# A recurrence solved in rounds: the passages between the rounds reordered on four engines

## What is computed

```python
# x: 6250 x 512, 100000 edges (src, dst), sorted by dst
x = x + gnn(layernorm(x), edges)        # segment sum, two dense layers
x = x + lstm(layernorm(x))              # one sequence of 6250 steps, hidden size 512
# the lstm's step, from h = c = 0:
#   f, i, o = sigmoid([x_t, h] @ W_* + b_*);  g = tanh([x_t, h] @ W_c + b_c)
#   c = f * c + i * g;   h = o * tanh(c)
```

## Time and profile before

| | us |
|---|---|
| median of three runs | 2959.19 (2956.31 to 2973.06) |
| the profiled execution | 2975.87 |
| its span, first to last instruction | 2974.3 |
| `lstm_part` in it | from about 1656 |
| mean granted TensorE clock | 0.942 |

### The profile page before, as it was taken

One profiled execution on the slowest core, in us unless ns is written; L12 is line 12 of the kernel. 1 busy time (PEld: TensorE's weight loads), 2 busy tenths in 40 slices (PEclk: granted clock), 3 DMA queues, 4 the chain that ended last, 5 costly groups with the idle time before them and its releaser, 6 DMA issues. The chain is left out here.

```text
span 2974.3 us, 47816 instructions
## 1 busy us (share of the span) xinstructions
PE 2593.7 (87%) x10746; PEld 1892.8 (64%) x10747; DVE 2149.9 (72%) x5785; ACT 1562.4 (53%) x3986; POOL 998.5 (34%) x1018
## 2 busy tenths in 40 slices
PE   7966888889888888897888799899999799989997
PEld 6845766667667666676666566666666555556654
DVE  7745767767677776676776588777777677778886
ACT  5643444444444444444443566566666477756775
POOL 0245556656566566565553100000000000003333
PEclk9977999989999999898999899999999899999999
DMA  9656777767777777676766766577787666659995
GB/s 240 181 147 193 218 208 226 217 196 222 211 213 217 218 214 215 195 223 197 217 207 194 187 190 177 168 242 237 235 243 237 168 165 168 170 157 253 251 252 148
DMA packets 194203, 611.10 MB, mean 205 GB/s; under 512 B 41822, under 2 KB 47966, under 8 KB 164394
## 3 DMA queue, kind: packets, MB, share of 16 engines
q1 hardware_dynamic: 120432, 370.08, 42.0%
q0 software_dynamic: 73712, 240.39, 29.4%
HBM read 468.71 MB, written 141.62 MB: 205 GB/s over the span
## 5 line engine op out<-in xcount | busy, mean ns | idle before, releaser
L823 POOL DMA_INDIRECT kept<-ln_table,kept x800 | 825.5, 1032 | 569.3 <-DVE shared L1030 324.7
L1518 PE MATMUL acc<-shared,state 128*125 128x512 f32 x2244 | 775.8, 416 | 61.6 <-DVE state L1814 46.2
L864 ACT ACTIVATE shared<-kept 128x512 fp32r<-128x512 f32 x800 | 445.2, 620 | 528.1 <-remote 310.4
L1518 PEld LDWEIGHTS acc<-shared,state 128*125 128x125 f32 x2244 | 401.3, 187 | 197.2 <-ACT acc L1449 64.9
L917 PE MATMUL agg<-shared,onehot 128*125 128x512 f32 x1200 | 431.9, 462 | 27.4 <-DVE shared L1030 18.8
L1359 POOL TENSOR_TENSOR out<-h,lx 125x512 f32<-125x512 f32 x50 | 64.5, 1290 | 1124.2 <-DVE h L1839 1124.2
L1518 PE MATMUL acc<-W_low,state 128*125 128x512 f32 x800 | 315.9, 395 | 0.0
L917 PEld LDWEIGHTS agg<-shared,onehot 128*125 128x125 f32 x1200 | 251.0, 218 | 100.8 <-issue 33.6
L1518 PE MATMUL acc<-last_high,state 128*125 128x512 f32 x748 | 298.8, 399 | 0.0
L1030 DVE TENSOR_TENSOR shared<-kept,shared 128x512 fp32r<-128x512 f32 x400 | 267.9, 689 | 14.9 <-ACT shared L864 6.7
L938 PE MATMUL gps<-Wx_high,zT_high 128*125 128x512 f32 x800 | 225.7, 405 | 49.7 <-ACT zT_high L899 33.7
(11 more groups left out here) (235 smaller groups left out, 4319.5 us busy)
## 6 DMA issues: line engine op xcount, KB each, us to landing
xg<-total_rows SPq DMA_DIRECT2D x100, 896.0 KB
xg<-gate_rows SPq DMA_DIRECT2D x88, 896.0 KB
gate_rows<-gout SPq DMA_DIRECT2D x200, 224.0 KB
total_rows<-total SPq DMA_DIRECT2D x50, 896.0 KB
kept<-ln_table,kept POOLq DMA_INDIRECT x800
lx<-x_rows POOLq DMA_DIRECT2D x50, 250.0 KB, 7.4
out_dram<-out POOLq DMA_DIRECT2D x50, 250.0 KB, 2.9
held<-in_x_dram SPq DMA_DIRECT2D x25, 448.0 KB
```

Of the source, the lines that this page charges most:

```text
L823: e.indirect_dma_start(out=rows[j % RING][:, :], out_offset=None, in_=table[:, :], in_offset=bass.IndirectOffsetOnAxis(ap=ends[:, b, j, 0: ...
L864: e.activation(high[j % PARTS][:, :], rows[j % RING][:, :], ACT.Copy).then_inc(s_high, 1)
L1518: m = e.matmul(acc[n][0:L, :], stationary[:, k, :], weights[k][:, n * PAIR:(n + 1) * PAIR], start=begins, stop=(k == K - 1), skip_group_ch ...
```

## The change

It changes seven things:

1. The check after `kept` is no longer made in the passage. Its h gaps are taken at two places (`gaps_of_h`), and its reductions (`loose_check`) stand on VectorE behind the new `state`. The loose verdict is scaled into a fifth column of `most`, which the last check takes into its maximum; the turn by TensorE and the comparison after `kept` are gone.
2. The ends are turned in another order: after `change`, decay, gate, cell; otherwise cell, gate, decay. The cell has a semaphore of its own, `s_cell_ends`, which `gap` waits for; the scans wait for `s_ends`.
3. In the last check the h gaps and their reductions stand before the cell gap, and fewer waits stand between them.
4. `back` is copied into `c` by ScalarE; `s_begin` counts three for each passage.
5. The first two of the four row additions that begin `change` and `final` stand on TensorE right behind the transposes of `c_start`.
6. For them row 0 is loaded earlier: for `change` by SyncE before the last store of `kept`, for `final` one step earlier.
7. `s_taken` is the first semaphore that TensorE increments at the part's beginning.

The diff, without the renumbered waits and a few plain lines:

```diff
@@ steps on SyncE @@
+                    if kind in ("change", "final"):
+                        if first and kind == "change":
+                            return
+                        e.wait_ge(s_taken, now - (2 if first else ROWS))
+                        load(s, q, totals_v)
+                        if first:
+                            hold(e, s_passed, s_taken, r * STEPS + AHEAD)
+                        return
...
                         if last:
+                            hold(e, s_passed, s_total_st[0], 2 * SPREAD)
+                            load(0, 0, totals_v)
                             store(s, q % 2)
@@ correct on ScalarE @@
                 e.activation(tc_start[:, :, :], c_start[:, :, :], ACT.Tanh).then_inc(s_tcs, 1)
+                e.wait_ge(s_ends, r * 2 + 2)
+                e.activation(c[0:L].rearrange("c k u -> c (k u)"), back[0:L, :], ACT.Copy).then_inc(s_begin, 1)
@@ TensorE @@
-            for s in (*s_acc, *s_turn, s_taken):
+            for s in (s_taken, *s_acc, *s_turn):
                 e.sem_inc(s, DONE)
...
-                            for n in range(4):
+                            for n in range(4) if kind == "rough" else range(2, 4):
                                 m = add_rows(n)
@@ measure on TensorE: cell, decay, gate before @@
+                if kind == "change":
+                    turn_faded()
+                    turn_gate().then_inc(s_ends, 1)
+                    turn_cell()
+                else:
+                    turn_cell()
+                    turn_gate()
+                    turn_faded().then_inc(s_ends, 1)
@@ correct on TensorE @@
                 t.then_inc(s_ends, 1)
+                if kind in ("kept", "change"):
+                    e.wait_ge(s_xg[0], rows_landed(r + 1, 0, 0))
+                    for bank in range(2):
+                        e.matmul(acc[bank][0:L, :], ident[0:L, 0:L], xg[0][0:L, 0, bank].bitcast(F32), start=True,
+                                 stop=False, skip_group_check=True)
@@ measure on VectorE @@
-                e.wait_ge(s_ends, r * 2 + 1)
+                if kind == "kept":
+                    gaps_of_h(r, kind, FIRST)
+                if checks is not None:
+                    gaps_of_h(r, kind, range(K))
+                    widest(h_gap, 2)
+                e.wait_ge(s_cell_ends, r + 1)
                 after_own(e.tensor_tensor(gap[:, :, 1:], turned[0][:, :, 0:L - 1], c_start[:, :, 1:], ALU.subtract))
                 if checks is None:
                     return
+                widest(gap, 0)
+                signed(1.0)
+                bounds = 5 if kind == "final" else 4
+                e.tensor_reduce(worst[:, :], most[:, 0:bounds], AX_X, ALU.max).then_inc(s_worst, 1)
...
+            def gaps_of_h(r, kind, ks):
                 of_h = hturned_half if kind == "kept" else hturned
+                for k in ks:
                     e.wait_ge(s_turn[k], (r + 1) * STEPS + AHEAD)
+                    beside_own(e.tensor_tensor(h_gap[:, k, 1:], of_h[k][:, 0:L - 1], h_start[:, k, 1:], ALU.subtract))
...
+            def widest(gaps, at):
+                e.wait_ge(s_own, base[0] + own[0])
+                for n, op in enumerate((ALU.max, ALU.min)):
+                    beside_own(e.tensor_reduce(most[:, at + n:at + n + 1], gaps[:, :, :].rearrange("p k l -> p (k l)"),
+                                               AX_X, op))
...
+            def loose_check():
+                widest(h_gap, 2)
+                widest(gap, 0)
+                signed(CELL_SHARE)
+                after_own(e.tensor_reduce(most[:, 4:5], most[:, 0:4], AX_X, ALU.max))
+                after_own(e.tensor_scalar(most[:, 4:5], most[:, 4:5], TOLERANCE / LOOSE, None, ALU.mult))
@@ correct on VectorE @@
+                e.wait_ge(s_ends, r * 2 + 1)
                 for k in range(K):
                     after_own(e.tensor_tensor_scan(change[:, k, 1:], turned[1][:, k, 0:L - 1], gap[:, k, 1:],
                                                    0.0, ALU.mult, ALU.add))
...
+                if kind == "kept":
+                    gaps_of_h(r, kind, SECOND)
+                    e.wait_ge(s_own, base[0] + own[0])
                 e.wait_ge(s_tcs, r + 1)
...
-                    after_own(e.tensor_tensor(state[:, :, :], h_start[:, :, :], begun, ALU.subtract))
+                    e.tensor_tensor(state[:, :, :], h_start[:, :, :], begun, ALU.subtract).then_inc(s_begin, 1)
...
-                e.wait_ge(s_ends, r * 2 + 2)
-                e.tensor_copy(c[0:L].rearrange("c k u -> c (k u)"), back[0:L, :]).then_inc(s_begin, 1)
-                e.wait_ge(s_begin, r * 2 + 3)
+                if kind == "kept":
+                    loose_check()
+                e.wait_ge(s_begin, r * 3 + 4)
```

More of the change, by code:

```diff
@@ L1176, in lstm_part @@
         tc_start = sb(ctx, "tc_start", [P, K, L])
-        most = sb(ctx, "most", [P, 4])
+        most = sb(ctx, "most", [P, 5])
         worst = sb(ctx, "worst", [P, 1])
@@ L1265, in all_rounds @@
                 steps(r, kind)
-                measure(r, kind, {"kept": 0, "final": 1}.get(kind))
+                measure(r, kind, 0 if kind == "final" else None)
                 if kind != "final":
@@ L1278, in all_rounds @@
                         steps(m + ROUNDS, "more")
-                        measure(m + ROUNDS, "more", m + 2)
+                        measure(m + ROUNDS, "more", m + 1)
                         correct(m + ROUNDS, "more")
@@ L1299, in steps, with load @@
                     hold(e, s_passed, s_sum[3], r * STEPS + AHEAD)
+                def load(s, q, rows_v):
+                    spread(e, xg[q][0:L].rearrange("c a b g -> c (a b g)").bitcast(F32), rows_v[s], s_xg[q])
                 def step(s, q, first, last):
                     now = r * STEPS + s + (AHEAD + 1)
-                    if kind in ONE_PASS:
+                    if kind in ("change", "final"):
[6 more added lines that the diff above has]
+                        return
+                    if kind == "rough":
                         e.wait_ge(s_taken, now - (1 if first else ROWS))
@@ L1306, in step @@
                         e.wait_ge(s_sum[3], now - (1 if first else ROWS))
-                    rows_v = totals_v if kind in ("change", "final") else gates_v
-                    spread(e, xg[q][0:L].rearrange("c a b g -> c (a b g)").bitcast(F32), rows_v[s], s_xg[q])
+                    load(s, q, gates_v)
                     def store(s, par):
@@ L1715, in measure @@
                 now = (r + 1) * STEPS + AHEAD
-                for k in range(K):
-                    e.wait_ge(s_c[k], now)
                 for half in range(2):
@@ L1724, in measure, with turn_cell, turn_faded, turn_gate @@
                     turned, one, cell, faded, gates = ends, ident, c, decay, gate
[L1725 to L1733, removed]
+                def turn_cell():
+                    for k in range(K):
+                        e.wait_ge(s_c[k], now)
+                        t = e.transpose(turned[0][:, k, :], cell[0:L, k], one[0:L, 0:L])
+                    t.then_inc(s_cell_ends, 1)
+                    return t
+                def turn_faded():
+                    if kind not in ("change", "final"):
+                        e.wait_ge(s_decay, now)
+                    for k in range(K):
+                        t = e.transpose(turned[1][:, k, :], faded[0:L, k // KH, (k % KH) * P:(k % KH + 1) * P],
+                                        one[0:L, 0:L])
+                    return t
+                def turn_gate():
+                    for k in range(K):
+                        t = e.transpose(turned[2][:, k, :], gate_of(k, 1, 1, gates), one[0:L, 0:L])
+                    return t
+                if kind == "change":
[6 more added lines that the diff above has]
+                    turn_faded().then_inc(s_ends, 1)
                 if checks is not None:
```

46 lines of the change are left out of this document (20 added, 26 removed).

## The result

| | us |
|---|---|
| before, median of 17 runs | 2963.59 (2954.46 to 2973.06) |
| after, median of 17 runs | 2944.69 (2929.70 to 2958.93) |
| ratio after to before | 0.9935, 95% interval 0.9921 to 0.9950 |
| span of the profiled execution | 2942.3, before 2974.3 |

The change saves 0.65%, 18.9 us by the medians. The forecast was 17.2 us and 0.58%.

What follows compares the result with a forecast made beforehand. In the passages between rounds and the closing check one engine works while others wait. B 6.9+1.5, C 1.0+1.5, A 2.1, D 2.2, start 1.0, clock 1.0: 17.2 us off 2959.2 gives 2942 us, range 2931 to 2953.

Steps and rivals of the forecast that it cites:

- B up to the scans: Passage from kept to change: scans start at 2315.12 instead of 2322.05, 6.9 us; about 5.8 the check, the rest order.
- Early additions: Starts of change and final: first two row additions directly follow the transposes of `c_start`, saving 1.5 us in each.
- ScalarE's copy: Copy of c in the passages: 0.60 us on ScalarE, 0.69 on VectorE; by the skill page's rule 2.1 us.
- A and C: A (rough to kept): 2.1 us, 1.4 to scans and 0.7 from the copy; C (change to final), to scans: 1.0.
- D: Closing check at the end: `apart` at about 2962.35 instead of 2964.58, 2.2 us saved, bounds 0 and 2.2.
- Start: Part's beginning: `s_taken` ahead of eight increments lets SyncE issue its first load earlier, 1.0 us, bounds 0 and 1.0.
- The deferred check: kept's check, behind the new state on VectorE: costs nothing; as a rival, not hidden, 3.8 us given back, chance 0.03.
- The clock: TensorE's low clock after the passages' pauses rises earlier, gaining 1.0 us in all, bounds -0.7 and 3.0.
- The end moved with D: Rival: POOL's drain keeps its end, start load no sooner, clock gives nothing; 13.0 us saved, 2946, chance 0.26.
- that rival: Rival: the clock stays up from change to final, 2.3 us more, 19.5 saved; 2939 with B's best; chance 0.12.
- price of moved code: Rival: moved code makes TensorE's 36 loop jumps after passage A dearer; at 1 us each 19 us slower, 2978, chance 0.04.
- The earlier loads of row 0: SyncE's queue: row 0 issued before kept's last store, and one step earlier in final; cost nothing.

Runs made afterwards that it cites:

- order_back: Changed kernel with ends turned in the old order and the cell gap waiting for all twelve; to the scans A 3.03, B 4.78, C 1.74, D 6.90 us.
- late_adds: Changed kernel with all four row additions at the rounds' beginning, behind the new state; B 12.80, C 12.00 us; scans to first addition 4.68 and 4.60.
- dve_copy: Changed kernel with VectorE copying `back` into `c` behind the state; A 6.84 us (+0.6), first additions 3.54 us after the scans, as in `after`.
- changed_again: Changed kernel unedited, timed a second time on one chip with best and the kernel before; median 2925.76 us, ratio to before 0.9957 (0.9929 to 0.9985).
- warm_more: Changed kernel, VectorE's eleven increments moved, eight unused matmuls per passage and six in kept's last step; A's first gate after 11.13, B 8.44, C 7.50 us.
- late_warm: warm_more with all four row additions at the rounds' beginning; B 10.18, C 9.14 us, the additions 3.13; A's first gate after 12.68.
- best: warm_more again, timed on one chip with changed_again and the kernel before; median 2920.43 us, ratio to before 0.9921 (0.9890 to 0.9953).
- inc_moved: Changed kernel with VectorE's eleven increments at the end of final moved into the branch for further rounds; D 5.92 us, 0.99 less; B 12.14, C 10.07.

## Why the prediction was right

**The gains are where the brackets were.** B up to the scans: 6.9 forecast, 7.6 measured. The 0.7 too little is the clock: I took all twelve transposes at the price of before, 2.73 us, when the clock had fallen at 2312.4, ahead of them. They now follow the last turns without a hole, and the clock fell at 2299.1, within them: 2298.33 to 2300.35, 2.0 us. order_back's 1.9 for the order, where I had 1.1, has the same source; it leaves 5.7 for the check, where I had 5.8.

**Early additions: 1.5 each, measured 1.8.** By late_adds 1.1 of this are the place and 0.7 the copy that VectorE no longer makes ahead of them; by dve_copy the copy costs nothing once the additions are early. The first addition does not wait until the last transpose's modelled end; it starts 1.06 us after `c_start`, not 1.3.

**ScalarE's copy.** 0.60 us in each passage, as the nearest row had it, so the bound drawn from the Trainium skill's page "ScalarE: Activation LUTs", section "Rules for kernel authors" (simple elementwise work to VectorE, up to about three times faster there in bf16) is not what this fp32 copy does; VectorE's took 0.69. Where the copy lies on the path, in A, its move gave 0.6 of the 0.7 foreseen.

**A and C.** 2.1 and 1.0 forecast, 2.2 and 0.9 measured. For C the reason was only partly right: order_back shows that the order gives 0.34; the rest comes from turning the cell's chunks as they end. The 1.0 of the prediction thus had the right size and the wrong source in more than half of it.

**D: 2.2 forecast, 2.1 measured, by errors that cancel: luck.** I had VectorE begin the h gaps at 2955.95 in the times of before; the eleven increments in front of them, hidden then behind TensorE's transposes, made it 0.79 later. Against that, the instructions without a wait between them run closer, 0.87 for the h gaps and 1.25 for a pair of reductions: gaps and reductions took 4.13 us together, where I had 4.75. The steps behind them took 1.50, where I had 1.65. The term was right in size and wrong in make. No run puts the old arrangement of this check back; the reading rests on these rows.

**Start: 1.0 forecast, 0.6 to 0.7 measured.** The wait of 1.0 us was not all to be had. SyncE has increments of its own, and was not ready at TensorE's first: its first load was issued 0.7 us after that increment, before 1.3, and the profile now shows no wait of it for TensorE.

**The deferred check.** It costs nothing, as forecast; its cover was 2.5 us and not the 4 that I had, since the first gate itself comes earlier when the additions do.

**The clock: 1.0 forecast.** In the profiled execution of the result it was 2.8 in the additions, less 0.4 in A. Over the seven executions with early additions and unfilled pauses (some with another edit elsewhere), the four additions took 4.88 us in B (3.99 to 5.62) and 4.74 in C (4.21 to 5.12); in the two with late ones, 5.60 and 5.56. That makes about 0.7 and 0.8, in a scatter of 1.6 from one execution to the next. In B the two groups overlap (5.34 and 5.86 late, up to 5.62 early), so with two executions on one side the gain is likely, and its size an estimate. What this pair of traces shows beyond the forecast is mostly such a scatter: B shrank by 11.3 us from the last h to the first product, where 8.4 were foreseen without the clock. The 2.9 more are 1.9 of the additions' clock, 0.7 of the transposes' and 0.3 of the early start.

**The rivals.** The end moved with D: POOL's drain was 8290 ns in both. The clock fell in C in every execution without filled pauses, so that rival didn't occur; filled, the pause kept it up. The loops' jumps back on TensorE are as before, 76 to 225 ns, so no price of moved code. No addition waits on a load.

```profile
L1253 PEldq COMPARE_BRANCH  x45: 76/215/225, 1678.8 to 2915.8; - x45
```

The earlier loads of row 0 were not tested alone.

The sum, then, was right within its terms' errors: 17.2 forecast, 19.4 from this pair of traces, 18.9 from the medians, whose interval reaches from 15 to 23. The mechanisms were the foreseen ones for 13 of the 17 us (B to the scans, the early additions in B and C, A, the start). That the total came out within 2 us is luck in part: the errors in D cancelled, the start gave 0.3 less and the clock more, and the second timing (0.9957) puts the gain anywhere from 4 to 21 us.

## What to carry to other kernels

Between two loops one engine works at a time, and the idle brackets of the timeline price each piece of the passage: add them by hand, engine by engine, and write down what each was hiding. When a wait is taken away, look at what the waiting engine does in front of it; here eleven increments, free for as long as transposes were awaited, became 0.9 us. And where a change is 0.6% and the runs of one kernel spread over 1%, stretches between two named instructions tell more than the whole.

## What the runs showed of the hardware

- A pause of TensorE of about 3 us can cost nearly as much again after it. The four row additions took 3.03 us when the clock stayed up (warm_more) and 3.99 to 5.62 in two executions of the changed kernel; all four at the round's beginning, 3.13 (late_warm) and 5.13 to 5.99 (before, late_adds).
- Filling the pauses with matmuls whose results nobody reads (fourteen in B, eight in A and C) made B and C 2.0 to 3.7 us and 1.7 to 2.5 us shorter (warm_more and best) than in the two executions of the changed kernel. In A the clock fell all the same: in three of four executions 1.3 to 1.5 us after the last pair of h began, and it rose 1.3 to 1.5 us before the first product; in the fourth (late_warm) it fell 0.8 us after the first product and rose 4.2 us after it.
- A semaphore increment is not free on the path: VectorE's come 0.1 us apart (eleven: 0.87 us), TensorE's 0.15 us apart (nine, 1656.3 to 1657.5).
- POOL's last drain took 8290 ns in `before`, `after`, changed_again and inc_moved alike, whether its last store had been issued 7.7 us before the drain began (`before`), 5.7 us (`after`) or 4.7 us (inc_moved).
